# Decoder layer in float32 on one core: partition exchange on VectorE, a fourth buffer of probabilities, units in other slots

## What is computed

```python
x = x + attn(layernorm(x))                 # 16 heads of 64, rotary on q and k, softmax, @ Wo
x = x + xattn(layernorm(x), ctx, mask)     # 16 heads of 64, queries masked by a row vector, @ Wout + bout
x = x + ffn(layernorm(x))                  # 8 experts 256 -> 256; gates = top 2 of softmax(x @ Wg), renormalised
# rotary, on interleaved pairs of the head's dimension:
re = xe * cos - xo * sin
ro = xe * sin + xo * cos
```

## Time and profile before

| | |
|---|---|
| runs | 3839.14, 3843.31, 3844.49 us (median 3843.31) |
| profiled execution | 3839.38 us, span in the trace 3837.6 us |
| TensorE clock granted | 0.992 on average |
| busy, share of the span | PE 92%, ACT 61%, DVE 58%, POOL 55% |
| bytes moved by DMA | 113.5 MB, mean 30 GB/s |

### The profile page before, as it was taken

One profiled execution on the slowest core, in us unless ns is written; L12 is line 12 of the kernel. 1 busy time (PEld: TensorE's weight loads), 2 busy tenths in 40 slices (PEclk: granted clock), 3 DMA queues, 4 the chain that ended last, 5 costly groups with the idle time before them and its releaser, 6 DMA issues.

```text
span 3837.6 us, 88277 instructions
## 1 busy us (share of the span) xinstructions
PE 3547.3 (92%) x29120; PEld 2973.7 (77%) x29120; DVE 2232.2 (58%) x6569; ACT 2342.5 (61%) x6698; POOL 2126.6 (55%) x1928
## 2 busy tenths in 40 slices
PE   3899999999999999999999999999999999999998
PEld 3777787777787777887777787778777777877786
DVE  4466555565565665555655656556556556566564
ACT  4665666556666665666656666556656566565573
POOL 3555665556655556655556655566555566555661
PEclk9999999999999999999999999999999999999999
DMA  4000010000000000100000000001000000000000
GB/s 137 23 23 28 28 33 26 25 25 28 30 32 25 25 25 28 33 29 23 24 31 28 32 25 25 25 28 33 29 23 24 31 28 32 25 25 25 28 33 6
DMA packets 85758, 113.54 MB, mean 30 GB/s; under 512 B 16192, under 2 KB 49472, under 8 KB 85312
## 3 DMA queue, kind: packets, MB, share of 16 engines
q1 hardware_dynamic: 84608, 107.30, 8.2%
q10 hardware_dynamic: 704, 0.27, 0.0%
HBM read 32.03 MB, written 8.39 MB: 11 GB/s over the span
## 4 chain that ended last, share of the span: by engine, by line
PE 55%; POOL 17%; issue 14%; DVE 9%; ACT 3%; DMA 1%; POOLq 0%; DVEq 0%; ACTq 0%; SPq 0%
PE unit_ps L476 13%; PE unit_ps L486 9%; PE oT_ps L596 8%; POOL probs L1058 7%; PE pT_ps L579 7%; PE score_ps L563 6%; PE wo_ps L620 6%; POOL rope L1070 4%; POOL swap L1066 4%; PE unit_ps L464 4%; DVE neg_max L851 2%; PE unit_ps L495 1%; DVE xn L804 1%; DVE g_exp L837 1%; ACT probs L730 1%
## 5 line engine op out<-in xcount | busy, mean ns | idle before, releaser
L1058 POOL TENSOR_TENSOR probs<-probs,inv_sum 128x512 f32<-128x512 f32 x1024 | 1062.7, 1041 | 1082.5 <-DVE inv_sum L845 1081.2
L719 ACT ACTIVATE pT<-pT_ps 128x512 f32<-128x512 f32 x1024 | 603.0, 592 | 117.3 <-PE pT_ps L579 117.3
L730 ACT ACTIVATE probs<-score_ps,neg_max 128x256 f32<-128x256 f32 x1024 | 475.3, 473 | 309.5 <-DVE neg_max L851 309.5
L730 ACT ACTIVATE probs<-probs,neg_max 128x256 f32<-128x256 f32 x1024 | 509.3, 500 | 224.5 <-DVE probs L862 222.0
L579 PE MATMUL pT_ps<-ident,probs 128*128 128x128 f32 x4096 | 632.8, 281 | 13.4 <-POOL probs L1058 13.3
L579 PEld LDWEIGHTS pT_ps<-ident,probs 128*128 128x128 f32 x4096 | 453.2, 142 | 221.4 <-issue 185.8
L862 DVE TENSOR_SCALAR_CACHE_REDUCE probs<-score_ps,mask_add 128x256 f32<-128x256 f32 x1024 | 448.4, 480 | 249.4 <-PE pT_ps L579 132.4
L596 PE MATMUL oT_ps<-pT,v_sb 128*64 128x256 f32 x4096 | 560.1, 395 | 7.8 <-ACT pT L719 7.8
L476 PE MATMUL unit_ps<-xs_hi,w_lo 128*128 128x256 f32 x1536 | 471.3, 307 | 53.8 <-DVE xs_lo L868 46.9
L851 DVE TENSOR_REDUCE neg_max<-score_ps 128x2 f32<-128x512 f32 x512 | 327.2, 679 | 306.8 <-PE score_ps L563 306.8
L476 PE MATMUL unit_ps<-xs_hi,w_hi 128*128 128x256 f32 x1536 | 438.9, 286 | 0.0
(11 more groups left out here) (115 smaller groups left out, 8568.6 us busy)
## 6 DMA issues: line engine op xcount, KB each, us to landing
swap<-raw SPq DMA_DIRECT2D x512, 128.0 KB, 2.0
x_in<-dram_x SPq DMA_DIRECT2D x32, 256.0 KB, 3.0
xn<-dram_ctx SPq DMA_DIRECT2D x32, 256.0 KB, 2.9
layer_out<-x SPq DMA_DIRECT2D x32, 256.0 KB, 2.2
swap<-dram_bout SPq DMA_DIRECT2D x32, 128.0 KB, 3.1
probs<-dram_ckv SPq DMA_DIRECT2D x6, 256.0 KB, 3.9
probs<-dram_we SPq DMA_DIRECT2D x4, 256.0 KB, 3.8
pT<-dram_we SPq DMA_DIRECT2D x4, 256.0 KB, 3.8
```

The lines of the kernel that those rows point to most:

```text
L719: nc.scalar.activation(flat(pT[:, s % 2, :, :]), pT_ps[s % 2][:], ACT.Copy).then_inc(pT_ready.sem, 1)
L730: last = nc.scalar.activation(dst, src, ACT.Exp, bias=neg_max[:, h % STATS, t:t + 1], scale=1.0 if h < H else -1.0, accum_out=row_sum[:, h ...
L1058: nc.gpsimd.tensor_tensor(weights, weights, inv.unsqueeze(2).to_broadcast([P, NT, T]), ALU.mult).then_inc(probs_ready.sem, 1)
```

## The change

Five edits, and a new placement:
- The exchange of odd and even partitions is made by `stream_shuffle` on VectorE, from the unit's PSUM bank to `swap`, right after the product with the cosines. `raw`, its copy on ACT and the DMAs go away. The scale of Q goes into the weights as they are staged.
- `P_BUFS` is 4: `probs` has four buffers, and the exponentials wait for the head of slot s-4. The ring for staging has six buffers.
- The logits are made with a weight matrix of 16 columns, high and low part side by side (`wg_both`): per token tile and half of the width two matmuls instead of three. DVE adds the two column groups.
- The experts' bias has 64 rows (56 of zeros) and lies in `rope`; `gatesT` is read with 64 rows.
- Units, norms, mask, gate table and projections have other slots.

```diff
-P_BUFS = 3
+P_BUFS = 4
 UNITS = {
-    0: [("Q", 2, 0, NOW)],
-    1: [("V", 0, 0, NOW)],
-    2: [("K", 2, 0, LATE)],
-    3: [("V", 1, 0, LATE)],
-    4: [],
-    5: [("Q", 3, 0, LATE)],
-    6: [("V", 2, 0, NOW), ("L3", 0, -1, NOW)],
+    0: [("Q", 2, 0, LATE)],
+    1: [],
+    2: [("V", 0, 0, NOW), ("K", 2, 0, LATE)],
+    3: [],
+    4: [("Q", 3, 0, LATE)],
+    5: [("V", 1, 0, NOW)],
+    6: [("V", 2, 0, LATE), ("L3", 0, -1, NOW)],
     7: [("LG", 0, -1, NOW)],
-    8: [("K", 3, 0, LATE)],
-    9: [("EX", 0, -1, LATE)],
-    10: [("EX", 1, -1, NOW), ("EX", 2, -1, LATE)],
-    11: [("V", 3, 0, NOW)],
+    8: [("K", 3, 0, LATE), ("EX", 0, -1, LATE)],
+    9: [],
+    10: [("EX", 1, -1, LATE), ("EX", 2, -1, LATE)],
+    11: [("GT", 0, -1, LATE), ("V", 3, 0, NOW)],
     12: [],
-    13: [("K", 4, 0, NOW), ("GT", 0, -1, NOW)],
+    13: [("K", 4, 0, NOW)],
...
-    18: [("EX", 5, -1, NOW), ("K", 5, 0, NOW), ("V", 4, 0, LATE), ("EX", 6, -1, LATE), ("L2", 0, 0, LATE)],
+    18: [("EX", 5, -1, NOW), ("K", 5, 0, NOW), ("V", 4, 0, NOW), ("EX", 6, -1, LATE), ("L2", 0, 0, LATE)],
...
-    22: [],
+    22: [("K", 6, 0, LATE)],
     23: [("V", 5, 0, NOW)],
-    24: [("K", 6, 0, LATE)],
-    25: [("Q", 6, 0, NOW)],
+    24: [],
+    25: [("Q", 6, 0, LATE)],
...
-    33: [("V", 7, 0, NOW)],
+    33: [("V", 7, 0, LATE)],
 AT = {
-    "gate table": 9,
+    "gate table": 8,
-    "mask": 8,
+    "mask": 4,
-    "norm 2": [18, 4],
+    "norm 2": [18, 2],
-    "statistics 1": 24,
-    "norm 1": 25,
+    "statistics 1": 25,
+    "norm 1": 26,
-    "projection first": [3, 7, 31],
+    "projection first": [7, 11, 27, 31],
 }
+def bias_first(s):
+    return s % 2 == 0 and UNITS[s] and UNITS[s][0][0] == "BI"
...
-        be_sb = raw[0:E, 0, 0:D]
-        gatesT, bout_sb = swap[0:E, 0, 0:T], swap[:, 1, 0:D]
+        be_sb = rope[0:HD, 0, 0, 0:D]
+        gatesT, bout_sb = swap[0:HD, 0, 0:T], swap[:, 1, 0:D]
...
     def read_signal(kind, g):
             if kind in ("Q", "K") and g < NG:
-                return cos_done, order_of(kind, g) + 1
+                return swapped, order_of(kind, g) + 1
-                    ... "LG": (gate_exp, 1),
+                    ... "LG": (logits_read, 2),
...
-            def swap_halves(b, kind, g, off):
-                n = order_of(kind, g)
-                sp.wait_ge(roped.sem, roped.at(b, off, n))
-                sp.wait_ge(raw_ready.sem, raw_ready.at(b, off, n + 1))
-                for i in range(2):
-                    sp.dma_start(swap[i::2], raw[1 - i::2]).then_inc(swapped.sem, 16)
...
                 elif kind == "LG":
                     for t in range(NT):
-                        last = tile_product(ps[:, t * E:(t + 1) * E], t, wg_hi, wg_lo, 0, E)
+                        c0 = 2 * t * E
+                        for c in range(NC):
+                            tokens = slice(t * P, (t + 1) * P)
+                            nc.tensor.matmul(ps[:, c0:c0 + 2 * E], xf_hi[:, c, tokens], wg_both[:, c, :], ...)
+                            last = nc.tensor.matmul(ps[:, c0:c0 + E], xf_lo[:, c, tokens], wg_both[:, c, 0:E], ...)
...
+                    if bias_first(s) and exists(b, UNITS[s][0][2]):
+                        unit(b, s, 0, *UNITS[s][0][:3])
...
             def unit(b, ps, kind, g, off):                       # ACT
-                elif kind in ("Q", "K") and g < NG:
-                    act.wait_ge(swapped.sem, swapped.at(b, off, n))
-                    act.wait_ge(projected.sem, projected.at(b, off, g + 1))
-                    nc.scalar.activation(flat(raw[:]), ps, ACT.Copy, ...).then_inc(raw_ready.sem, 1)
...
-                back = next(head_in(s - i) for i in (3, 6, 9) if head_in(s - i))
+                back = next(head_in(s - i) for i in (4, 8, 12) if head_in(s - i))
...
             def cosines(b, ps, kind, g, off):                    # DVE
-                dve.wait_ge(raw_ready.sem, raw_ready.at(b, off, n + 1))
+                dve.wait_ge(projected.sem, projected.at(b, off, g + 1))
+                dve.wait_ge(roped.sem, roped.at(b, off, n))
...
+                nc.vector.tensor_tensor(rope[:, n % 2, :, :], ps.rearrange("p (c t) -> p c t", c=NC), cos,
+                                        ALU.mult).then_inc(cos_done.sem, 1)
+                nc.vector.stream_shuffle(flat(swap[:]), ps, [i ^ 1 for i in range(32)]).then_inc(swapped.sem, 1)
...
                 elif kind == "LG":                               # DVE
-                    nc.vector.tensor_reduce(g_nmax[:], ps[:, 0:NT * E]..., AX.X, ALU.max, negate=True)
+                    nc.vector.tensor_copy(g_logit[:], both[:, :, 0:E]).then_inc(logits_read.sem, 1)
+                    nc.vector.tensor_tensor(g_logit[:], both[:, :, E:2 * E], g_logit[:], ALU.add).then_inc(logits_read.sem, 1)
+                    nc.vector.tensor_reduce(g_nmax[:], g_logit[:], AX.X, ALU.max, negate=True).then_inc(gate_max.sem, 1)
```

More of the change, by code:

```diff
@@ L128 @@
 }
-TURN = 2
-SPLIT = 3
 FLAT = [u for s in range(SLOTS) for u in UNITS[s]]
@@ L147 @@
 AT = {
+    "turn": 2,
+    "split": 3,
     "statistics 3": 4,
@@ L353, in q_scale @@
         def q_scale(g):
-            return SCALE if g < NG else -SCALE
+            return 1.0 if g < NG else -SCALE
         def pieces(hi, lo):
@@ L396, in _ @@
         def _(sp):
-            for j, (src, _, _) in enumerate(STAGES):
+            for j, (src, _, _, _) in enumerate(STAGES):
                 slot = j % len(stages)
@@ L528, in unit @@
                     for t in range(NT):
-                        last = tile_product(ps[:, t * E:(t + 1) * E], t, wg_hi, wg_lo, 0, E)
+                        c0 = 2 * t * E
+                        for c in range(NC):
+                            tokens = slice(t * P, (t + 1) * P)
+                            nc.tensor.matmul(ps[:, c0:c0 + 2 * E], xf_hi[:, c, tokens], wg_both[:, c, :],
+                                             start=c == 0, stop=c == NC - 1, skip_group_check=True)
+                            last = nc.tensor.matmul(ps[:, c0:c0 + E], xf_lo[:, c, tokens], wg_both[:, c, 0:E],
+                                                    start=False, stop=c == NC - 1, skip_group_check=True)
                     last.then_inc(logits_done.sem, 1)
@@ L637, in body @@
                     for n, (kind, g, off, _) in enumerate(UNITS[s]):
-                        if exists(b, off):
+                        if exists(b, off) and not (n == 0 and bias_first(s)):
                             unit(b, s, n, kind, g, off)
@@ L689, in unit @@
                     for t in range(NT):
-                        last = nc.scalar.activation(g_exp[:, t, :], ps[:, t * E:(t + 1) * E], ACT.Exp,
+                        last = nc.scalar.activation(g_exp[:, t, :], g_logit[:, t, :], ACT.Exp,
                                                     bias=g_nmax[:, t:t + 1], accum_out=g_sum[:, t:t + 1])
@@ L758, in body @@
                         nc.scalar.activation(flat(ct_hi[:]), flat(xn[:]), ACT.Copy).then_inc(ctx_hi_ready.sem, 1)
-                    for kind, g, off in rotated(s, SPLIT):
+                    for kind, g, off in rotated(s, AT["split"]):
                         if exists(b, off):
@@ L1060, in body @@
                             ALU.mult).then_inc(probs_ready.sem, 1)
-                    for kind, g, off in rotated(s, TURN):
+                    for kind, g, off in rotated(s, AT["turn"]):
                         if exists(b, off):
```

62 lines of the change are left out of this document (28 added, 34 removed).

## The result

The kernel after takes 3685.1 us (median of 4 runs, 3678.7 to 3687.5), the kernel before 3841.2 (4 runs beside it). The ratio is 0.9588, 95% interval 0.9574 to 0.9603: 156 us faster, where 99 were forecast. The profiled execution took 3678.7 us with a span of 3676.9.

The account below looks back on a forecast made before the run. TensorE's own sequence plus its holes was taken as the bound. Banks 39.7 + 39.7, logits 14.2, slots 22 to 24 21.1, less 15.5 of new waits, gave 99.2 us gained: 3744 us, range 3712 to 3805.

Parts of the forecast that it names:

- Both banks: Slots 6 and 10: L3 and EX2 no longer wait for banks that DVE frees late; 39.7 us gained at each.
- The shuffle's length: New VectorE shuffle of 512 columns from PSUM, 256 times: 0.75 us each with its mask.
- more columns in the gate: Gate logits: a 16-column matmul costs the same as an 8-column one; even doubled, 0.4 us per body lost.
- the waits for probabilities and for pT: Slots 22 to 24: TensorE's waits of 13.3 and 7.8 us go, 21.1 us gained.
- the change leaves alone: Slot 0: TensorE's largest hole, read as the loop's turn, stays as before at about 71 us.
- Fourth buffer ... 0 more: Cross-attention: DVE's maxima need no turn of the slot before, but TensorE hardly waits for them; no further gain.
- The staging term: Staging with six buffers instead of five: within 3 us of zero, both ways.
- None is waited for by TensorE, so the gain in the sum is 0: Exchange: removing ACT's 256 copies, 512 DMAs and the waits for them gains TensorE nothing.
- the 0.5 us a body of new waits: Late points in slots 4 to 7, 23 and 27: 0.5 us lost per body, 15.5 us in all.
- The rival of the port: Slot 8: POOL's work stretches DVE's gate chain, head 8's turn 0.75 us late; 23 us lost, 3767 us, chance 0.12.
- The slower rival: Shuffle of 2.37 us delays maxima and bank releases on DVE, 5.3 us per body; 3893 us, chance 0.10.
- fit, by 0.6 us: Slots 8 and 9: head 8's reciprocal and K3's shuffle (before EX1 takes its bank) are in time by 0.6 us.

Follow-up runs that it names:

- e6: e1 with the low part of the attention output put between VectorE's two row maxima from slot 22 on; 3694.4 us, ratio 0.9610.
- e10: The kernel after with two bodies in each turn of the loop; 3649.1 us, ratio 0.9472.
- e1: The kernel after with three buffers of probabilities instead of four, and five for staging; 3739.7 us, ratio 0.9732.
- e4: The kernel after with three buffers and the old slots, leaving the exchange on VectorE, wide logits and 64-row bias; 3840.4 us, ratio 1.0.
- e2: The kernel after with units, norms, mask, gate table and projections in the slots of before; 3819.8 us, ratio 0.9942.
- e3: The kernel before with the new slots alone (exchange by DMA, three buffers, old logits); 3818.7 us, ratio 0.9948.
- e8: e1 with ACT again copying each projected Q and K, VectorE's steps waiting for the copy; 3816.0 us, ratio 0.9934.
- e7: The kernel after with the cosine product before each shuffle done twice, so each exchange ends later; 3744.2 us, ratio 0.9746.
- e5: The kernel after with logits in three matmuls per chunk and the bias product on 8 rows, as before; 3692.4 us, ratio 0.9610.

## Why the forecast was too small

A body was forecast 3.2 us shorter (99.2 / 31) and is 4.86. The 1.66 between them are 0.71 at the loop's turn, 0.5 of new waits that did not come, 0.21 in slots 0 to 6, 0.21 in the bias product's pair, 0.15 at the two banks and 0.08 in 30 to 32, less 0.18 in 22 to 26, to rounding.

**Right.** Both banks: 8 to 14 is 1.38 shorter (1.28 forecast), and 6 to 8 1.78 (1.28 and 0.45 for the logits). The shuffle's length, no gain or loss by more columns in the gate, xs_lo unchanged, and DVE at 62% (65 forecast: the norms and some of the small operations took 127 us less in all). Slots 22 to 26 gave 0.50 instead of 0.68: the waits for probabilities and for pT did not go, but fell from 13.3 and 7.8 to 8.9 and 2.5 us.

**Wrong: the loop's turn "the change leaves alone".** I had found the right cause and drawn a wrong conclusion from it. The sequencer's own records (not in the rows above) have TensorE's branch at 3.63 us before and 3.60 after, on average over 29 turns, and 0.36 us from its end to the scores. The branch did not change. At the end of the loop, where it is not taken, its record is 0.08 us. What changed is what TensorE still has in work meanwhile. It can't reach the branch before the last projection's wait for `oT_lo` is met. Before, `oT_lo` ended at 1929.18 (the first timeline under e6), the projection began at once, and its 1.6 us are all that covers the branch up to the scores at 1933.12. TensorE's timeline before:
```profile
1928.82 0.60 PE L579 MATMUL pT_ps<-ident,probs 128*128 128x128 f32 x4
1929.23 0.39 PE L620 MATMUL wo_ps<-w_hi,oT_lo 128*128 128x256 f32 x1
```
After, `oT_lo` ends at 1850.05, while TensorE is still at the K projection and has the turn of a head's probabilities before it. The projection begins 0.85 us later, and all of it lies over the branch:
```profile
1850.55 0.60 PE L582 MATMUL pT_ps<-ident,probs 128*128 128x128 f32 x4
1850.90 0.36 PE L623 MATMUL wo_ps<-w_hi,oT_lo 128*128 128x256 f32 x1
...
1854.61 0.39 PE L566 MATMUL score_ps<-k_lo,q_both 64*128 64x256 f32 x2 [2.03 <-POOL q_both L1050]
```
Over the 29 turns that is 0.78 us more cover, less 0.16 by which the branch starts later behind `oT_lo` (0.37 us instead of 0.21): the hole is 1.81 us instead of 2.45. The pair 34 to 0 is 0.71 shorter, 0.08 of it busy time, which makes 21 us. e10 shows that the hole belongs to the turn, e6 that the place of `oT_lo` sets it. The Trainium skill, Advanced Engine Details and Errata, "Control Flow Timing", gives a compare-and-branch about 108 ns; measured is 3.6 us where it is taken. The Trainium skill, Runtime: NRT & Kernel Launch, "Instruction fetch mechanics", says that a taken branch to a target outside the window that is loaded must first fetch it. It gives no length, and no run here was made to separate the fetch from the rest, so the cause of the 3.6 us stays open. What the other engines' traces show speaks for it: the price of a taken branch changes there with the length of the loop. From the branch to the sequencer's next record VectorE takes 0.27 us before and 2.77 after, ScalarE 3.41 before and 0.20 after, GpSimd 0.22 in both, while the instructions in the trace per body are 310 and 334, 344 and 323, and 124 and 116; that is argued, not tested. TensorE's scores come 0.36 us behind its own branch in both kernels, so they wait for none of these three.

**Wrong: "Fourth buffer ... 0 more".** I looked for TensorE waiting on the maxima and found none. But the maximum's wait holds up what is queued behind it on VectorE, `oT_lo`, and for that TensorE waits. By e1 the term is 55 us with the new slots (most of the turn's 21 us above is part of it), 21 with the old ones; by e6 45 of the 55 are the place of `oT_lo`, at the loop's turn and in 26 to 28, whose projection now comes first in slot 27. With the old slots (e4 to e2) only the turn gets shorter, 8.24 to 7.64, while 6 to 8 gets 0.43 longer. The staging term, 3.3 us, lies a little outside its bound of 3.

**Wrong: the exchange, "None is waited for by TensorE, so the gain in the sum is 0".** With the old slots it costs what logits and bias bring, since e4 is at 1.0 with them: about 0.6 us a body, mostly at Q3's bank. With the new slots it is the removal of ACT's copy that makes them possible: new slots with the copy 3819 (e3) and 3816 (e8), without it 3740 (e1). I had priced the parts against the kernel before, one by one, and not in the new order. There V0, which covers the copy of Q2 and head 1's exponential behind it, has moved to slot 2. With the copy still there, more than half of the 80 us of the two banks is given back: in e3 slots 0 to 2 and 4 to 6 take 1.31 us more together than before, and 6 to 8 gives 0.83 instead of 1.28. e8 puts the place of the copy at 1.20 us a body (0 to 2); its other 0.99, in 6 to 8 and 28 to 30, can be the copy's place or the later shuffle.

**Wrong: the 0.5 us a body of new waits.** None came; L528 waited for xf_lo once, 1.5 us, as the gate's product did once before. I had laid norm 3 out with the 1.17 us an operation of the earlier trace rows, and it ran at 0.93, but what that alone gave wasn't tried. The rival of the port went the other way: of the norm operations fewer met one of POOL's (62 instead of 93), and small gate operations shortened as well (the product of the probabilities from 710 to 436 ns).

**Small terms.** The bias product with its entry gives 0.21 us a body, where I had 0.1 either way. Fewer half-clock stretches give another 0.2, which is what slots 0 to 6 gained.

**The slower rival** wanted a shuffle of 2.37 us and was to decide from 1.8 on; the shuffle takes 0.742, so its condition isn't met. e7 tests its price: with 1.4 us for second product and shuffle the time is 3744, still 96 below before, so the threshold lies above 1.4; whether at 1.8 isn't shown. Of its walk, K3's bank and head 8's turn "fit, by 0.6 us" is borne out, as 8 to 14 stays at 18.91 in e7. The cost starts elsewhere, and at once above 0.74 us: in 6 to 8, and at Q0's bank, which the walk had late for a shuffle of 2.37 us alone.

## What to carry to other kernels

Price a part of a change in the order that the whole change makes, not in the order of before: here the exchange (with logits and bias) is worth 0 alone and the new slots without it 21 us, but both together 101. A move can also bare a wait that was there all along: see what work covers it. A wait that costs TensorE nothing can hold up the next operation in its own engine's queue; look at that one. The hole at a loop's turn is the branch less the work that is already released in front of it, so the last wait before the branch sets it; either have its input ready earlier, or turn less often.

## What the runs showed of the hardware

After the idle time at the loop's turn TensorE's granted clock sometimes falls to its lower level, 1.2 GHz, while the scores and products of slot 0 run. In the kernel after this happens at 6 of the 29 turns, before at 10, in e6 at 11, in e1 at 13; in e10 at 2 of 14. TensorE was idle for 1.8 to 2.1 us ahead of it in the kernel after, 2.2 to 2.8 before. Two stretches of the kernel after (columns: busy us and count of PE, PEld, DVE, ACT, POOL, then the granted clock, DMA's share, GB/s):
```profile
1740.90:1744.40 3.50, 3.47 (x21) 2.14 (x22) 1.62 (x4) 1.02 (x4) 2.76 (x3) 0.53 0.02 7
1845.00:1850.00 5.00, 5.00 (x48) 4.20 (x46) 3.70 (x13) 3.48 (x9) 5.00 (x5) 1.00 0.00 0
```
In the first the eight products with values take 1.97 us; elsewhere they take 1.08. One such stretch costs about 1.5 us in slots 0 to 2, which take 5.92 us on average with it and 4.38 without. Why it comes at some turns and not at others stays open: the idle times of those without it, 1.5 to 2.1 us in the kernel after, overlap with the others.

The bias product with 64 rows starts 0.09 us after the scores ahead of it, the one with 8 rows 0.21 us, and its matmuls take 376 instead of 400 ns on average: adding rows of zeros made it cheaper, by 0.21 us for the pair 20 to 22 (e5).
